# Attention to neighbours' keys: products straight from PSUM, products of weights and values on GpSimd

## What is computed

```python
q, k, v = (x @ wq + bq), (x @ wk + bk), (x @ wv + bv)        # each (n, 8, 16)
score = einsum('ehd,egd->ehg', q[A], k[B])
ssum  = segment_sum(score, A);  cnt = segment_sum(ones, A)
score = softmax(ssum / maximum(cnt, 1.0)[:, None, None], axis=-1)
out   = einsum('ehg,egd->ehd', score, v).reshape(n, 128) @ wo + bo
```

## Time and profile before

| what | value |
|---|---|
| median of 3 runs | 2545.51 us |
| profiled execution, whole | 2553.13 us |
| its span | 2551.3 us |
| TensorE busy in the span | 2136.5 us (84%) |
| VectorE | 2075.0 us (81%) |
| ScalarE | 1777.5 us (70%) |
| GpSimd | 88.5 us (3%) |
| mean granted TensorE clock | 0.928 |

### The profile page before, as it was taken

How to read it: one execution, slowest core, us unless ns; L and a number is a source line. 1 busy time by engine, 2 the same in 40 slices (tenths; PEclk the granted TensorE clock), 3 DMA queues, 4 the chain that set the end, 5 groups by cost and what they waited for, 6 DMA issues and landing times. The chain is left out here.

```text
span 2551.3 us, 89583 instructions
## 1 busy us (share of the span) xinstructions
PE 2136.5 (84%) x34184; PEld 1883.2 (74%) x34184; DVE 2075.0 (81%) x4498; ACT 1777.5 (70%) x3000; POOL 88.5 (3%) x138
## 2 busy tenths in 40 slices
PE   3799999799799799596967899879998899877746
PEld 3555555599699699495957889779997898867724
DVE  6799999788788787616169999899999999959953
ACT  5799999766666666202048999799997999746522
POOL 2211111000000000000000000000000000000000
PEclk8899999999899899798988999999999999988868
DMA  4244555543243342182812333123322333034200
GB/s 107 103 206 206 212 212 212 213 131 116 85 136 103 103 131 90 65 258 65 258 65 72 103 91 97 55 88 110 110 82 59 102 99 93 27 119 140 64 0 25
DMA packets 178872, 294.13 MB, mean 115 GB/s; under 512 B 6383, under 2 KB 158834, under 8 KB 178590
## 3 DMA queue, kind: packets, MB, share of 16 engines
q1 hardware_dynamic: 177802, 288.86, 34.2%
q0 software_dynamic: 800, 1.26, 0.2%
HBM read 205.62 MB, written 84.47 MB: 114 GB/s over the span
## 5 line engine op out<-in xcount | busy, mean ns | idle before, releaser
L1175 ACT ACTIVATE relmsk<-relad,relthr 125x625 bf16 (+1 forms) x1080 | 770.8, 811 | 19.4 <-DVE relsel L1232 18.8
L1382 PE MATMUL ps<-relmv,relsel 125*128 125x66 f16 x15000 | 734.9, 196 | 34.2 <-DVE relsel L1232 28.8
L1382 PEld LDWEIGHTS ps<-relmv,relsel 125*128 125x128 f16 x15000 | 683.5, 100 | 52.3 <-DVE relsel L1232 31.0
L1386 PE MATMUL ps<-relmv,relct 125*128 125x132 f16 x3750 | 543.2, 229 | 1.7 <-issue 1.7
L1232 DVE TENSOR_TENSOR relsel<-relmsk,relct 125x1920 f16<-125x1920 bf16 (+1 forms) x375 | 422.7, 1127 | 12.4 <-ACT relmsk L1175 12.4
L1227 DVE SCALAR_TENSOR_TENSOR relsel<-relad,relthr,relct 125x625 f16<-125x625 f16 (+1 forms) x420 | 357.6, 860 | 7.9 <-DVE relnum L1261 4.7
L453 ACT ACTIVATE stage<-ps 125x375 f32 x625 | 313.8, 602 | 37.6 <-PE ps L393 33.4
L346 DVE TENSOR_SCALAR col<-iota_col,window_col 125x376 bf16<-125x376 f16 x1250 | 308.4, 316 | 15.4 <-PE ps L393 15.4
L393 PE MATMUL ps<-col,lo 125*125 125x375 bf16 x1250 | 290.2, 345 | 16.4 <-DVE col L346 16.2
L1386 PEld LDWEIGHTS ps<-relmv,relct 125*128 125x128 f16 x3750 | 246.1, 99 | 1.9 <-issue 1.8
L393 PEld LDWEIGHTS ps<-col,lo 125*125 125x125 bf16 x1250 | 136.8, 139 | 143.4 <-DVE col L346 140.6
(11 more groups left out here) (476 smaller groups left out, 2792.1 us busy)
## 6 DMA issues: line engine op xcount, KB each, us to landing
counts<-stage SPq DMA_DIRECT2D x75, 800.0 KB, 4.8
ct<-counts_all SPq DMA_DIRECT2D x75, 800.0 KB, 4.7
relct<-counts SPq DMA_DIRECT2D x75, 800.0 KB, 4.8
counts_all<-total SPq DMA_DIRECT2D x25, 800.0 KB, 7.3
stage<-counts_all SPq DMA_DIRECT2D x25, 800.0 KB, 4.5
g1ct<-counts_all SPq DMA_DIRECT2D x25, 800.0 KB, 4.6
g2ct<-counts_all SPq DMA_DIRECT2D x25, 800.0 KB, 4.6
relad<-ad_rows SPq DMA_DIRECT2D x12, 1250.0 KB
```

The source lines that it names most:

```text
L1175: act.activation(msk[:, s % 5, n, :, 0:P], ad[:, bass.ds(g % 2, 1), h] .rearrange("p a (b d) -> p (a b) d", d=PAD)[:, :, 0:P], ACT.Relu, b ...
L1382: pe.matmul(K.ps[:, b, 2 * h * F:2 * (h + 1) * F], sel[:, s % 5, h, b], vs[:, (h * 2 + p) * 2 * F:(h * 2 + p + 1) * 2 * F], start=False, s ...
L1386: ins = pe.matmul(K.ps[:, b, 0:2 * HF].rearrange("p (h a f) -> p h a f", h=H, a=2)[:, :, 1], ct[0:P, s // 5, b, s % 5], vs[:, (4 + p) * HF ...
```

## The change

Six edits, all in `attend_to_keys`:

1. VectorE no longer copies the gathered keys to `kl`. It multiplies q by the sums in PSUM; counts and `span` are applied afterwards to the 64 scores of a block. TensorE subtracts the own key with two more matmuls per block, of a matrix `minus` and the block's own `parts`.
2. Five buffers `pr` instead of two; all five products of a chunk are issued first and then the sums. TensorE's wait for `drained` becomes a wait for the product of the same bank (`mult`).
3. GpSimd makes the products of weights and values of chunks 0 to 3 in five buffers `wv`, after VectorE's weights (`weighted`). VectorE sums them (`sum_values`) in the next chunk, one behind each sum of scores. The last chunk's products stay on VectorE.
4. `s` has two halves, by the chunk's parity.
5. ScalarE makes the exponentials after move 20, not 18.
6. `cT` is not cleared, and its stationary slice is 125 columns wide, not 128. VectorE's loop over chunks is written out.

```diff
-    EXP_AT = 18
-    LINKS = 6
+    EXP_AT = 20
+    LINKS = 7
+        def weigh(eng, c, b, to):
+            return eng.tensor_tensor(to[:, b].rearrange("p (h d g) -> p h d g", h=H, d=DH),
+                                     s[:, c % 2, b].unsqueeze(2).to_broadcast([P, H, DH, H]),
+                                     qkv[:, 5 * c + b:5 * c + b + 1, 2 * D:3 * D].rearrange("p a (d g) -> p a d g", d=DH)
+                                     .to_broadcast([P, H, DH, H]), ALU.mult)
...
                 Q.over_partitions(pool)
+                for c in range(4):
+                    pool.wait_ge(weighted, c + 1)
+                    for b in range(5):
+                        pool.wait_ge(summed, 5 * c + b + 1)
+                        weigh(pool, c, b, wv).then_inc(weighed, 1)
...
                             if t < 5:
-                                pe.wait_ge(drained, 5 * c + t + 1)
+                                if not first:
+                                    pe.wait_ge(mult, 5 * c + t - 4)
+                                for p in range(2):
+                                    pe.matmul(K.ps[0:P, j, 0:W], minus[:], parts[:, bass.ds(5 * c + j, 1), p, 0:W]
+                                              .rearrange("p a f -> p (a f)"), start=(p == 0), stop=False)
                             for b in range(5):
                                 for p in range(2):
-                                    ins = pe.matmul(K.ps[:, j, 0:W], cT[0:P, t % 5, b], parts[:, 5 * g + b, p],
-                                                    start=(g == 0 and b == 0 and p == 0),
+                                    ins = pe.matmul(K.ps[0:P, j, 0:W], cT[0:P, t % 5, b, 0:P], parts[:, 5 * g + b, p],
+                                                    start=False,
                                                     stop=(g == 4 and b == 4 and p == 1))
...
-                v.memset(cT[:], 0.0).then_inc(cleared, 1)
+                v.tensor_scalar(minus[:], K.ident16[0:P, 0:P], -1.0, None, ALU.mult).then_inc(cleared, 1)
...
+                def scores_of(c, earlier):
+                    link = Chain(v, own, LINKS * c)
+                    sc = s[:, c % 2]
                     v.wait_ge(used, 25 * c + 30)
+                    link(v.tensor_scalar(cnt[:], K.ps[0:P, 0:5, D], 1.0, None, ALU.max))
                     for b in range(5):
+                        v.wait_ge(red, 5 * c + b + 1)
+                        v.tensor_tensor(pr[:, b].rearrange("p (h g d) -> p h g d", h=H, g=H),
+                                        qkv[:, 5 * c + b:5 * c + b + 1, 0:D].rearrange("p a (h d) -> p (a h) d", h=H)
+                                        .unsqueeze(2).to_broadcast([P, H, H, DH]),
+                                        K.ps[0:P, b, 0:D].rearrange("p (g d) -> p g d", g=H).unsqueeze(1)
+                                        .to_broadcast([P, H, H, DH]), ALU.mult).then_inc(mult, 1)
+                        if b == 1:
+                            link(v.reciprocal(cnt[:], cnt[:]))
+                        if b == 3:
+                            link(v.tensor_scalar(cnt[:], cnt[:], span, None, ALU.mult))
+                    for b in range(5):
+                        v.wait_ge(mult, 5 * c + b + 1)
+                        v.tensor_reduce(sc[:, b], pr[:, b].rearrange("p (h g d) -> p h g d", h=H, g=H),
+                                        AX.X, ALU.add).then_inc(red, 1)
+                        if earlier:
+                            v.wait_ge(weighed, 5 * (c - 1) + b + 1)
+                            sum_values(c - 1, b, wv)
+                    v.wait_ge(red, 5 * c + 10)
+                    s5 = sc.rearrange("p b h g -> p b (h g)")
+                    link(v.tensor_tensor(s5, s5, cnt[:].unsqueeze(2).to_broadcast([P, 5, H * H]), ALU.mult))
+                    link(v.tensor_reduce(m[:], sc, AX.X, ALU.max))
...
+                for c in range(5):
+                    scores_of(c, c > 0)
+                v.wait_ge(weighted, 5)
+                for b in range(6):
+                    if b < 5:
+                        weigh(v, 4, b, pr).then_inc(mult, 1)
+                    if b > 0:
+                        v.wait_ge(mult, 25 + b)
+                        sum_values(4, b - 1, pr)
```

More of the change, by code:

```diff
@@ L1569, in attend_to_keys @@
         cnt = sb("cnt", [P, 5], F32)
-        kl = sb("kl", [P, 5, D], F32)
-        pr = sb("pr", [P, 2, H * H * DH], F32)
-        s = sb("s", [P, 5, H, H], F32)
+        minus = sb("minus", [P, P], F16)
+        pr = sb("pr", [P, 5, H * H * DH], F32)
+        wv = sb("wv", [P, 5, H * H * DH], F32)
+        s = sb("s", [P, 2, 5, H, H], F32)
         m = sb("m", [P, 5, H], F32)
-        (turned, moved, used, drained, cleared, own, mult, red, centred, exped, turns) = (S(tag + "_" + n) for n in (
-            "turned", "moved", "used", "drained", "cleared", "own", "mult", "red", "centred", "exped", "turns"))
+        (turned, moved, used, cleared, own, mult, red, centred, exped, weighted, weighed, summed) = (
+            S(tag + "_" + n) for n in ("turned", "moved", "used", "cleared", "own", "mult", "red", "centred", "exped",
+                                       "weighted", "weighed", "summed"))
         made, taken, unit = (S(tag + "_" + n) for n in ("made", "taken", "unit"))
@@ L1687, in _ @@
                     Q.low(v, q)
-                with v.Fori(0, 5) as c:
+                v.sem_inc(summed, 5)
+                def scores_of(c, earlier):
                     link = Chain(v, own, LINKS * c)
-                    heads = lambda first, b: qkv[:, bass.ds(5 * c + b, 1), first:first + D] \
-                        .rearrange("p a (h d) -> p (a h) d", h=H)
+                    sc = s[:, c % 2]
                     v.wait_ge(used, 25 * c + 30)
+                    link(v.tensor_scalar(cnt[:], K.ps[0:P, 0:5, D], 1.0, None, ALU.max))
@@ L1720, in _ @@
                     link(v.reciprocal(m[:], m[:]))
-                    link(v.tensor_tensor(s[:], s[:], m[:].unsqueeze(3).to_broadcast([P, 5, H, H]), ALU.mult))
-                    for b in range(6):
-                        if b < 5:
-                            v.wait_ge(red, 10 * c + b + 6)
-                            v.tensor_tensor(pr[:, b % 2].rearrange("p (h d g) -> p h d g", h=H, d=DH),
-                                            s[:, b].unsqueeze(2).to_broadcast([P, H, DH, H]),
-                                            qkv[:, bass.ds(5 * c + b, 1), 2 * D:3 * D]
-                                            .rearrange("p a (d g) -> p a d g", d=DH)
-                                            .to_broadcast([P, H, DH, H]), ALU.mult).then_inc(mult, 1)
-                        if b > 0:
-                            v.wait_ge(mult, 10 * c + 5 + b)
-                            v.tensor_reduce(att[:, bass.ds(5 * c + b - 1, 1)].rearrange("p a (h d) -> p (a h) d", h=H),
-                                            pr[:, (b - 1) % 2].rearrange("p (h d g) -> p h d g", h=H, d=DH),
-                                            AX.X, ALU.add).then_inc(red, 1)
@@ L1735, in _, with sum_values @@
-                    assert link.n == LINKS
+                    v.tensor_tensor(sc, sc, m[:].unsqueeze(3).to_broadcast([P, 5, H, H]), ALU.mult).then_inc(weighted, 1)
+                    assert link.n == LINKS
+                def sum_values(c, b, of):
+                    v.tensor_reduce(att[:, 5 * c + b].rearrange("p (h d) -> p h d", h=H),
+                                    of[:, b].rearrange("p (h d g) -> p h d g", h=H, d=DH),
+                                    AX.X, ALU.add).then_inc(summed, 1)
```

30 lines of the change are left out of this document (5 added, 25 removed).

## The result

| | before | after |
|---|---|---|
| median | 2544.81 us (4 runs, 2541.6 to 2546.17) | 2516.34 us (4 runs, 2515.17 to 2519.72) |
| profiled execution, span | 2551.3 us | 2514.0 us |
| TensorE busy | 2136.5 us (84%) | 2138.6 us (85%) |
| VectorE busy | 2075.0 us (81%) | 2044.0 us (81%) |
| GpSimd busy | 88.5 us (3%) | 123.6 us (5%) |

The ratio is 0.9887, with an interval of 0.9862 to 0.9911: 28.5 us less. The direction was right; the size was not. Of the 12.3 us that were missed, 2.3 lie in the attention stage and 6.7 at the start of the program; the rest is of the size by which the same kernel's savings differ from one timing to the next.

A forecast was written before the change was run, and what follows sets the result against it. VectorE was taken to set attention's pace at 30.8 us a chunk, TensorE afterwards at 24.3. With edges, loads, first use, scaling and a longer last chunk, the stage ended 16.2 us earlier: 2545.5 - 16.2 = 2529.3 us, range 2520 to 2547.

The forecast's parts named there:

- first chunk ready, against before: Attention's start: dropping the clearing of cT gains 0.25 us, ten unhidden extra matmuls in chunk 0 cost 0.9: +0.65 us.
- TensorE's period without additions, with loads: TensorE's attention chunk: period 24.3 us, plus 0.3 a period for loads of the narrower stationary operand.
- step 0 behind the chunk before: TensorE's chunk start: ScalarE's table load and move let step 0 begin 2.5 us after the chunk before ended.
- scaling beside GpSimd, extra: VectorE's scaling of counts by span waits for GpSimd's current product: 1.2 us in chunks 2 to 4, 3.6 in all.
- last chunk: Attention's last chunk on VectorE, with ten value products: 33.5 us plus 1.2 of scaling, where it was 30.5.
- (b): TensorE's attention matmuls are bound by loads of 125 columns: 2566 us at 35 ns, 2550 half-shown; chance 0.13.
- (c): VectorE's products and sums with one SBUF operand also contend with GpSimd in the attention chunks: 2555 us; chance 0.09.
- (d): GpSimd's value products are slow on runs of 8, 4.3 us each: 2542 us; chance 0.09.
- Rival (e): TensorE's clock falls in the new gaps, three slow steps a chunk: 4 us, 2533 us; chance 0.08.
- One sign: At a chunk's start, ScalarE, not VectorE, would stand behind TensorE's gaps.
- first use: GpSimd's first value product waits for 8.6 us of loading behind the wait for the weights: 1.3 us, once.
- Rival (a): No blocking of the scaling, and GpSimd loads ahead of the wait: 3.6 + 1.3 us come back, 2524.4; chance 0.13.

The follow-up runs named there:

- after_again: The changed kernel unchanged, timed again beside other kernels on one chip: 2521.7 us, ratio 0.9929 to the kernel before.
- after_3: The changed kernel unchanged, timed again in the third group: 2518.4 us, ratio 0.9893 to the kernel before.
- a_fold2: Second timing of the changed kernel with the counts' scaling by span folded into the operation taking their maximum: 2518.6 us, ratio 0.9894 to the kernel before.
- b_last_tt2: Second timing of the kernel before with a tiny elementwise GpSimd operation behind its last reduction: 2539.5 us, ratio 0.9977 to the kernel before.
- a_last_reduce: The changed kernel with a tiny reduction over partitions behind GpSimd's last value products: 2526.7 us, ratio 0.9941 to the kernel before.
- b_again: The kernel before, unchanged, profiled once more: 2547.5 us, profiled span 2545.7 us.
- a_wide128: The changed kernel with stationary slices of 128 columns and cT cleared again: 2520.5 us, ratio 0.9909 to the kernel before.
- a_exp18: The changed kernel with the exponentials after move 18 as before: 2526.9 us, ratio 0.9937 to the kernel before.
- a_kl: The changed kernel with the sums copied to SBUF and the products reading both inputs there: 2543.6 us, ratio 1.0003 to the kernel before.
- a_values_dve: The changed kernel with the value products of chunks 0 to 3 on VectorE instead of GpSimd: 2550.1 us, ratio 1.0027 to the kernel before.

## Why the prediction was partly right

**What holds.** TensorE sets the pace after the change, and the periods came out as summed. Put beside each other, from TensorE's first product on:

| step of the sum | forecast | measured |
|---|---|---|
| first chunk ready, against before | +0.65 | +0.85 |
| TensorE's period without additions, with loads | 24.6 | 24.51 |
| product out of PSUM | 1.18 | 1.13 |
| step 0 behind the chunk before | 2.5 | 2.56 |
| GpSimd's product of 1024 | 2.33 | 2.34 |
| scaling beside GpSimd, extra | 1.2, three chunks | 0.69, 0.96, 0.68 and 0.88, four chunks |
| from the first chunk's begin to the fifth's | 102.1 | 100.87 |
| last chunk | 34.7 | 33.45 |
| stage | -16.2 | -18.5 |

The products are free of the shared path, GpSimd is hidden, and rivals (b), (c) and (d) are out by the runs above. Rival (e) happened once in four chunks, at 0.5 us (25.95 less 24.51 and less the scaling's 0.96), not the 4 us I gave it. In `after_again` and `after_3` it also struck chunk 0, at 1.4 us (25.89), and in `a_fold2` no chunk: that it stayed small is partly luck. One sign failed: the trace puts TensorE's gap of 1.78 us down to VectorE's product, where I had named ScalarE. By the times of the rows ScalarE came last (the first product of the pair ends near 2305.5, half way through 2.35 us; the table load ends at 2305.76 and the move behind it takes 0.69 more), so the sign was badly chosen, and the step began where the sum had it.

**Mis-sized terms in the stage**, 2.3 us together, by their place. The head cost 0.2 more than summed; that is this one profile, for in `after_again` and `after_3` the first chunk is ready 1.1 us sooner and its period is 1.4 longer, 0.3 more in all. The four periods cost 1.2 less: 1.3 of first use did not come, the base was 24.51 and not 24.6 (0.4 less), and the clock cost 0.5. The scaling's share was right as a sum, 2.3 against 2.4, and wrong in its parts: it was put at 1.2 in chunks 2 to 4 and at nothing in chunk 1; its rows are 0.23 us in chunk 0 and 0.92, 1.19, 0.91, 1.11 behind. `a_fold2` confirms it from the other side, 24.33 where there were 25.2. Rival (a) had said that five elements might pass. In the scaling they don't. But it is not all small instructions: the reciprocal of the same 125 x 5 numbers in SBUF (L1723) takes 0.18 us beside GpSimd's products as without them, in every chunk. The first use of GpSimd was put at 1.3 us and cost nothing, since the load came ahead of the wait. That half of rival (a) is what happened. The last chunk was 1.25 shorter than summed: 0.3 is the scaling, 0.25 the five products at 1.13 and not 1.18, and 0.4 the exponentials, for which I had raised the 2.5 us of the earlier trace rows to 3.0 (in chunk 1 it is 2.63, from 2323.49 to 2326.12); 0.3 is spread over the sums.

**The step that failed** is that the sum put everything outside the attention stage at nothing. "Stages behind the attention wait for all of `att` and move up by what is saved" was all that I allowed the change to do outside. But the change also replaced GpSimd's last instruction, a reduction over partitions, by an elementwise one, and an execution then begins without some 7.5 us of loading, of which 6.7 (5.6 to 7.3 in the pairs of profiles) reach the first comparison, on the path that leads to everything. I had a price in hand: the earlier trace rows show 8.63 us of loading between a reduction and an elementwise instruction. I used it for the stage and did not look at the start of the program, where GpSimd stood idle for 8.16 us before the iota with nothing named that it waited for, since no edit was near it. `b_last_tt2` (5.9 us less, 2.5 to 9.4 by its interval, from one tiny instruction) shows the price in time, and the starts at 8.49 and 1.08 us its place; `a_last_reduce` (5.0 more than the kernel beside it by the medians, 3.1 by the ratios) agrees, but its time alone would not decide.

With it the account closes. Against the mean saving of 25.0 us: 18.2 in the stage (18.5, and 17.9 between the undisturbed profiles) and 5.6 to 6.7 at the start (the first comparison in either pair) make 23.8 to 24.9, inside the intervals of all three timings. The 28.5 us of the result are some 4 to 5 more than that; no run gives them a cause, and the other two timings do not have them. Without the start the result would have been near 2523, inside the range.

**The 7.6 us** by which the profiled execution of before lay over its median I had put outside the stage, and taken the saving off the median. `b_again` shows that this was right: an instruction of GpSimd stood for 13.3 us in counting in the first profile and for 2.5 in this one. Had I taken the saving off the profile, the stall would have been counted as part of every run. What starts it is open: two of the fourteen profiles have such a stall. In the first of them VectorE's comparisons follow each other without a gap from 66.1 us to 101.8, and GpSimd's instruction ends 0.3 us behind them; but they follow each other without a gap in the profiles where it ends after 2.5 us too. Single executions some 10 us and more above their median stand in several groups (four of 21 of the kernel before in the first); whether they hold such a stall isn't shown, as they have no profile.

## To carry to other kernels

Before saying that the rest of a program is untouched, look at the first rows of each engine and at what each engine does last: some of GpSimd's state seems to cross the end of the program, and kernels with a reduction over partitions as GpSimd's last instruction started their counting stage 6.4 us later here. Work could be given to GpSimd beside VectorE because VectorE's large instructions were sums with one SBUF input and products with one SBUF and one PSUM input, none of which was slowed. One SBUF input is not enough as a rule: a scaling (`TENSOR_SCALAR`) of 125 x 5 numbers was blocked, and so were the comparisons of the earlier trace rows, while a reciprocal was not. The scaling was worth folding into an instruction that reads PSUM, which took 0.22 us. When a queue in order (here ScalarE's) holds both the pace engine's moves and the other's exponentials, the place of the latter has to be moved together with the length of the chunk: two moves too early cost 7.4 us, part of it by the longer blocking of the scaling.

## What the runs showed of the hardware that was not expected

- Kernels whose last GpSimd instruction is elementwise begin without a gap (iota at 1.08 us, ten profiles), and those that end in a reduction over partitions begin with some 7.5 us of it (8.27 to 8.61 us, four profiles). The gap in the other direction, ahead of `a_last_reduce`'s reduction, was 6.08 us.
- The request for the library (`MODIFY_POOL_CONFIG`) ran ahead of a wait: it stood at 2252.8 us for an instruction that could not begin before 2300.6.
- Beside GpSimd's 2.34 us products, a VectorE scaling of 125 x 5 numbers with its input in SBUF took 0.91 to 1.19 us instead of 0.23 (up to 1.29 in `a_wide128` and 2.08 in `a_exp18`), and pairs of products with two SBUF inputs 4.49 and 6.45 instead of 2.35, while sums with one input kept their 1.13 and a reciprocal of the same 125 x 5 numbers its 0.18.
- After the same 1.78 us of idling TensorE kept its speed at one chunk's start (2306.70) and lost it for three steps at the next (2331.91). After 5.26 us (`a_kl`) and 5.15 us (`a_values_dve`) it came back with steps of 1.66 us, at a granted clock of 0.50.
